# An LSTM step on one core: forget and input gate written to PSUM, and a copy of the cell in SBUF

## The chip, the cores and the metric

The kernel runs on one core of a Trainium2 chip. The metric is the device time of one execution, in microseconds. Before the change it is 229.61 us, the median of three runs (229.58 to 229.65).

## The reference

Two recurrent layers run over 128 time steps on 32 sequences with 128 features each, in fp32. Layer 0 is an LSTM, layer 1 a UGRNN cell; each adds its output to its input. Cut to what matters:

```python
# layer 0, per step; xW is x @ Wx + b
a = xw_t + prev_h @ Wh
i = sigmoid(a[:, :H]);  f = sigmoid(a[:, H:2*H]);  o = sigmoid(a[:, 2*H:3*H]);  g = tanh(a[:, 3*H:])
next_c = f * prev_c + i * g
next_h = o * tanh(next_c)
x = x + hs                                  # input of layer 1
# layer 1, per step
m = concatenate([xt, h]) @ weight + bias
g = sigmoid(m[:, :U] + 1.0);  c = tanh(m[:, U:])
h_new = g * h + (1.0 - g) * c
x = x + ys
```

## The kernel before

Everything is held transposed: the 128 features lie on the partitions, the 32 sequences in the free dimension, so each elementwise operation works on a tile of 128x32. The 128 steps run one after the other in Python-unrolled code, sixteen to a body (`BODY`), and every engine has its own list of instructions in program order. Only semaphores join the lists. No planner or scheduler moves anything. In the texts below "position k" of a step s is k = s modulo 8.

**One step s of layer 0.** TensorE adds `h(s-1) @ Wh` to sums that lie in PSUM, one bank for each gate (`gate_banks`, in the order f, i, g, o). The forget gate comes first, as one product in fp32 (`forget_sum`, L262); the other three are made of three products with `h_high` and one with `h_low` each (`high`, L268, and `low`, L272), in the order i, g, o. ScalarE follows with the sigmoid of f into `forget`, the sigmoid of i into every second element of `scan_mul`, the tanh of g into every second element of `scan_add`, and the sigmoid of o into `out_gate` (all L470, through `gates`). All four results lie in SBUF. VectorE's `keep` (L564) multiplies `forget` by the old cell, which it reads in the bank `cell_bank`, into the other elements of `scan_add`. `scan` (L570) is a `tensor_tensor_scan` over 64 elements that computes i*g + f*c and writes `cell_bank`. ScalarE's `state` (L489) takes the tanh of the cell into `tanh_c`, in the bank `act_bank` of PSUM, and VectorE's `hidden` multiplies it by the output gate, into `hT` (L577) and, scaled and in fp16, into `h_high` (L578). `hidden_low` (L584) makes `h_low`. With `hT` TensorE can begin the next step.

**Layer 1 lies one step behind.** ScalarE takes one tanh over 128x64 (L494, into `acts1`), VectorE makes two `pair1` rows (L591, L593), the new state (L599, `acts<-pair`) and its two remainders (L605 `u_rest`, L610 `u_low`); TensorE multiplies them (L288), each as soon as its part is there. VectorE's list in one step is: hT, h_high, x1T (L619, the sum that feeds layer 1), h_low, the two pair rows, outT (L627, the output), the layer-1 state, keep, u_rest, scan, u_low. `keep` and `scan` therefore stand behind four instructions that wait for layer 1.

**Work for later steps.** TensorE also computes `x @ Wx` for groups of steps ahead, one projection a step (`project0`, L230): into the bank of f at positions 0 and 1, of i at 2 and 3, of g at 4 and 5, of o at 6 and 7. It stands between L288 on `acts` and L288 on `u_rest`. A matmul must not write a bank that another engine is using, so it waits: at positions 0 and 1 for `f_ready` (the forget gate's activation is done), at 2 to 5 for `scan_in_ready` (counted by `keep` and by the activation of g), at 6 and 7 for `o_ready` (the output gate's activation is done). At positions 1 and 3, and at 0 of every second group, it waits for an input chunk (`x_in`) too.

SyncE loads x and stores the output, 64 KB at a time; nothing below depends on it.

Of the kernel before, what the change touches and what calls it, by code (L numbers as in the profile page):

```python
# [8 lines left out]
ACT = mybir.ActivationFunctionType  # L9

P = 128
# [29 lines left out]
def two_layer_recurrence(nc, xt, h_first, wx, wh, b, w1, out_t):  # L41
# [5 lines left out]
    with ctx:  # L47
        def sb(name, shape, dt=F32):
            return ctx.enter_context(nc.sbuf_tensor(name, shape, dt))

        def bank(name):
            return ctx.enter_context(nc.psum_tensor(name, [P, 512], F32))
# [33 lines left out]
        hT = sb("hT", [P, RING, N])  # L86
        h_high = sb("h_high", [P, PARTS, N], F16)
        h_low = sb("h_low", [P, PARTS, N], F16)
        scan_mul = sb("scan_mul", [P, N, 2])
        scan_add = sb("scan_add", [P, N, 2])  # L90
        forget = sb("forget", [P, N])
        out_gate = sb("out_gate", [P, N])


# [10 lines left out]
        cell_bank, act_bank = bank("cell_bank"), bank("act_bank")  # L105
        cell = cell_bank[:, 0:2 * N].rearrange("p (n two) -> p n two", two=2)
        tanh_c = act_bank[:, 0:N]
        a1 = [bank(f"a1_{i}") for i in range(2)]

        x_in = [sem(f"x_in{i}") for i in range(CHUNKS)]  # L110
# [115 lines left out]
        def _(pe):  # L226
# [28 lines left out]
            def first_state(q, done):  # L255

                nc.tensor.matmul(gate_step(q, 0), wh_raw[:, q * P:(q + 1) * P], condT[:, :],  # L257
                                 start=False, stop=True, skip_group_check=True).then_inc(done, 1)
# [7 lines left out]
            def high(q, j):  # L266
                for weights in parts_of(wh_scaled, wh_rest, wh_third, q - 1):
                    nc.tensor.matmul(gate_step(q, j), weights, h_high[:, (j - 1) % PARTS, :],  # L268
                                     start=False, stop=False, skip_group_check=True)
# [59 lines left out]
            bias0(GATE_G, 0, 5)  # L329
            pe.wait_ge(wh_in, 16)  # L330
            pe.wait_ge(cond_in, 16)
            first_state(GATE_I, i_summed)
            first_state(GATE_G, g_summed)
            project0(GATE_O, 0, 7)
            bias0(GATE_O, 0, 7)
            first_state(GATE_O, o_summed)
# [1 line left out]
            def body(s0, first, last):  # L338
                for j in range(BODY):
                    s, m, k = s0 + j, j // GS, j % GS  # L340
                    r, l = s - 1, (j - 1) % BODY
                    if not (first and j == 0):
                        pe.wait_ge(h_ready, s)
                        forget_sum(j)
                        if first and j == 1:
                            pe.wait_ge(wh_split, 2)
                        pe.wait_ge(high_ready, s)
                        high(GATE_I, j)
                        if first and j == 1:
                            pe.wait_ge(fp16_ready, 1)  # L350
                        pe.wait_ge(low_ready, s)
                        low(GATE_I, j, i_summed)
                        high(GATE_G, j)
                        low(GATE_G, j, g_summed)
                        high(GATE_O, j)
                        low(GATE_O, j, o_summed)
                        if first and j == 1:
                            pe.wait_ge(w1_gate_ready, 1)
                            project1(0, 0, 0, 0)
                            project1(1, 0, 0, 0)  # L360
                            bias1(0, 0)
                            pe.wait_ge(w1_scaled, 1)
                            pe.wait_ge(w1_split, 2)
                            pe.wait_ge(fp16_ready, 2)
                            layer1_input(l)
                            layer1_first()
                        else:

                            pe.wait_ge(acts1_ready, s - 1)
                            if first and j == 2:  # L370
                                project1(0, 0, 1, HS)
                                bias1(0, 1)
                                pe.wait_ge(w1_split, 4)
                            if first and j == 3:
                                project1(1, 0, 1, HS)
                            layer1_input(l)
                            layer1_high(r, l)
# [5 lines left out]
                    if k == 0:  # L383
                        if m == 0:
                            pe.wait_ge(x_in[0], s0 + 16)
                            pe.wait_ge(x_in[1], s0 + 16)

                        if not (first and j == 0):
                            pe.wait_ge(f_ready, s)
                        project0(GATE_F, a, a_steps)  # L390
                    if k == 1:
                        if not ends:
                            pe.wait_ge(x_in[2 if m == 0 else 4], s0 + 16)
                        pe.wait_ge(f_ready, s)
                        project0(GATE_F, b, b_steps, False)
                    if k == 2:
                        pe.wait_ge(scan_in_ready, 2 * s + 1)
# [50 lines left out]
        def _(act):  # L448
# [23 lines left out]
            def gates(s, j, first):  # L472
                if not first:
                    act.wait_ge(f_summed, s)
                    gate(forget[:, :], GATE_F, j, ACT.Sigmoid).then_inc(f_ready, 1)
                act.wait_ge(i_summed, s + 1)
                gate(scan_mul[:, :, 1], GATE_I, j, ACT.Sigmoid)
                act.wait_ge(g_summed, s + 1)
                gate(scan_add[:, :, 0], GATE_G, j, ACT.Tanh).then_inc(scan_in_ready, 1)
                if first:  # L480
                    act.wait_ge(w1_in, 16)
                    scale_input(0)
                    scale_input(1).then_inc(w1_scaled, 1)
                act.wait_ge(o_summed, s + 1)
                gate(out_gate[:, :], GATE_O, j, ACT.Sigmoid).then_inc(o_ready, 1)

            def state(s):
                act.wait_ge(cell_ready, s + 1)
                nc.scalar.activation(tanh_c[:, :], cell[:, :, 1], ACT.Tanh).then_inc(tanh_c_ready, 1)  # L489

            def layer1(r, j):
                i = (j - 1) % RING
# [22 lines left out]
        def _(dve):  # L515
# [6 lines left out]

            for slot in range(SLOTS):
                nc.vector.memset(blank[:, slot:slot + 1], 0.0).then_inc(out_free[slot], 16)
            nc.vector.memset(scan_mul[:, :, :].rearrange("p n two -> p (n two)"), 0.0)
            nc.vector.memset(scan_add[:, :, :].rearrange("p n two -> p (n two)"), 0.0).then_inc(zeros_ready, 1)
            then(nc.vector.memset(bias_lhs[:, :], 0.0))
            nc.vector.memset(bias_lhs[ONE_ROW:P, :], 1.0)
# [32 lines left out]

            def keep(s):
                dve.wait_ge(f_ready, s)
                nc.vector.tensor_tensor(scan_add[:, :, 1], forget[:, :], cell[:, :, 1],  # L564
                                        ALU.mult).then_inc(scan_in_ready, 1)

            def scan(s):

                dve.wait_ge(scan_in_ready, 2 * s + 1)
                nc.vector.tensor_tensor_scan(cell[:, :, :].rearrange("p n two -> p (n two)"),  # L570
                                             scan_mul[:, :, :].rearrange("p n two -> p (n two)"),
                                             scan_add[:, :, :].rearrange("p n two -> p (n two)"),
                                             0.0, ALU.mult, ALU.add).then_inc(cell_ready, 1)

# [137 lines left out]
```

## Time and profile before

| what | value |
|---|---|
| median of three runs | 229.61 us |
| span of the profiled execution | 227.5 us, so some 2.1 us of the time lie outside it |
| PE busy | 222.5 us (98%) |
| DVE busy | 200.2 us (88%) |
| ACT busy | 120.1 us (53%) |
| chain that ended last | DVE 79%, ACT 11%, PE 3% |

The busy shares are to be read with care: instructions of one engine overlap in the records. A VectorE instruction lasts some 0.19 us, and the next one on the engine starts some 0.10 to 0.12 us after it did. So two neighbours both count as busy, and an engine can wait for a tenth of a microsecond without an idle record. For a kernel of such small instructions the starts in the timeline say more than the busy time does. The TensorE clock was granted in full (0.997 of 2.4 GHz on average).

### The profile page before, as it was taken

To read this page: it belongs to the slowest core of one execution; us is meant where nothing else is said; L and a number is where in the kernel's file an instruction comes from. 1 tells how busy PE (TensorE), PEld (TensorE's weight loads), DVE (VectorE), ACT (ScalarE), POOL (GpSimd) and SP (SyncE) were. 2 spreads that over 40 slices of the span, in tenths; PEclk is the share of its full clock that TensorE was granted. 3 is DMA by queue.
4 is the path that set the end of the run, shared out by engine and by line. 5 is a ranking of instruction groups with operands and counts; after the bars stand their busy time and mean duration, and the time that the engine had idled before them with its cause. 6 is when DMAs were issued, how large, how long until landed. Compare 5 with 4: busy or idle time off the path is not lost.

```text
span 227.5 us, 12371 instructions
## 1 busy us (share of the span) xinstructions
PE 222.5 (98%) x4850; PEld 207.1 (91%) x4850; DVE 200.2 (88%) x1555; ACT 120.1 (53%) x775; POOL 3.7 (2%) x12
## 2 busy tenths in 40 slices
PE   7999999999999999999999999999999999999994
PEld 5899999999999999999999999999999999999883
DVE  5889889899899898998998989989989989899895
ACT  3555555555555555555555555555555555555551
POOL 2400000000000000000000000000000000000000
PEclk9999999999999999999999999999999999999998
DMA  6001001000010001000011100100001000000000
GB/s 191 23 13 27 19 23 49 17 25 27 20 45 26 26 16 50 26 16 26 26 39 26 27 18 23 49 14 27 27 23 42 26 26 16 27 14 16 14 14 14
DMA packets 12004, 6.69 MB, mean 29 GB/s; under 512 B 1446, under 2 KB 11692, under 8 KB 11948
## 3 DMA queue, kind: packets, MB, share of 16 engines
q1 hardware_dynamic: 11376, 5.33, 8.3%
q8 instruction: 38, 0.62, 1.2%
q10 hardware_dynamic: 572, 0.59, 0.7%
q14 instruction: 18, 0.15, 0.2%
HBM read 3.82 MB, written 2.10 MB: 26 GB/s over the span
## 4 chain that ended last, share of the span: by engine, by line
DVE 79%; ACT 11%; issue 4%; PE 3%; DMA 1%; ACTq 0%
DVE cell_bank L570 13%; ACT act_bank L489 10%; DVE hT L577 8%; DVE scan_add L564 8%; DVE x1T L619 7%; DVE acts L599 7%; DVE pair L591 7%; DVE h_high L578 6%; DVE u_rest L605 6%; DVE outT L627 6%; DVE pair L593 6%; DVE h_low L584 6%; DMA xT<-in_x_dram 1%; PE a L288 1%; PE a L316 0%
## 5 line engine op out<-in xcount | busy, mean ns | idle before, releaser
L262 PE MATMUL gate_f<-hT,wh_raw 128*128 128x32 f32 x254 | 48.0, 271 | 0.3 <-DVE hT L577 0.2
L262 PEld LDWEIGHTS gate_f<-hT,wh_raw 128*128 128x128 f32 x254 | 37.8, 188 | 11.0 <-DVE hT L577 9.3
L470 ACT ACTIVATE forget<-gate_f 128x32 f32<-128x32 f32 x127 | 25.1, 197 | 36.1 <-PE gate_f L262 36.1
L494 ACT ACTIVATE acts<-a 128x64 f32<-128x64 f32 x128 | 28.6, 223 | 29.2 <-PE a L288 28.3
L577 DVE TENSOR_TENSOR hT<-out_gate,act_bank 128x32 f32<-128x32 f32 x128 | 24.0, 187 | 20.9 <-ACT act_bank L489 20.9
L489 ACT ACTIVATE act_bank<-cell_bank 128x32 f32<-128x32 f32 x128 | 23.3, 182 | 35.2 <-DVE cell_bank L570 35.1
L570 DVE TENSOR_TENSOR_SCAN cell_bank<-scan_mul,scan_add 128x64 f32<-128x64 f32 x128 | 38.2, 298 | 0.1
L280 PE MATMUL a<-h_high,w1x_scaled 128*128 128x32 f16 x256 | 35.4, 176 | 0.3 <-DVE w1x_fp L560 0.2
L280 PE MATMUL a<-h_high,w1x_third 128*128 128x32 f16 x256 | 35.4, 176 | 0.0
L280 PE MATMUL a<-h_high,w1x_rest 128*128 128x32 f16 x256 | 35.4, 176 | 0.0
L282 PE MATMUL a<-h_low,w1x_fp 128*128 128x32 f16 x256 | 35.3, 176 | 0.0
L288 PE MATMUL a<-acts,w1h_scaled 128*128 128x32 bf16 x254 | 33.2, 181 | 0.0
L288 PE MATMUL a<-acts,w1h_rest 128*128 128x32 bf16 x254 | 32.1, 177 | 0.0
L288 PE MATMUL a<-acts,w1h_third 128*128 128x32 bf16 x254 | 32.0, 177 | 0.0
L288 PE MATMUL a<-u_rest,w1h_scaled 128*128 128x32 bf16 x254 | 29.3, 178 | 0.0
L288 PE MATMUL a<-u_rest,w1h_rest 128*128 128x32 bf16 x254 | 28.9, 177 | 0.0
L470 ACT ACTIVATE scan_mul<-gate_i 128x32 f32<-128x32 f32 x128 | 25.7, 201 | 0.7 <-PE gate_i L257 0.7
L288 PE MATMUL a<-u_low,w1h_scaled 128*128 128x32 bf16 x254 | 25.9, 178 | 0.1
L470 ACT ACTIVATE scan_add<-gate_g 128x32 f32<-128x32 f32 x128 | 25.7, 200 | 0.0
L280 PEld LDWEIGHTS a<-h_high,w1x_scaled 128*128 128x128 bf16 x256 | 24.8, 97 | 0.8 <-ACT w1h_scaled L466 0.4
L619 DVE TENSOR_TENSOR x1T<-hT,xT 128x32 f32<-128x32 f32 x128 | 25.3, 198 | 0.0
L470 ACT ACTIVATE out_gate<-gate_o 128x32 f32<-128x32 f32 x128 | 25.2, 197 | 0.1
(113 smaller groups left out, 1047.5 us busy)
## 6 DMA issues: line engine op xcount, KB each, us to landing
xT<-in_x_dram SPq DMA_DIRECT2D x45, 64.0 KB, 1.9
out_dram<-outT SPq DMA_DIRECT2D x32, 64.0 KB, 1.6
wx_s<-in_L_cond_Wx_dram SPq DMA_DIRECT2D x1, 256.0 KB, 2.8
wh_raw<-in_L_cond_Wh_dram ACTq DMA_DIRECT2D x1, 256.0 KB, 3.3
w_raw<-in_L_cond_weight_dram ACTq DMA_DIRECT2D x1, 256.0 KB, 3.4
xT<-in_x_dram ACTq DMA_DIRECT2D x1, 64.0 KB, 3.3
bias_rows<-in_biases_dram ACTq DMA_DIRECT2D x1, 3.0 KB
condT<-in_cond_dram SPq DMA_DIRECT2D x1, 16.0 KB, 3.1
```

The costliest lines, as they stand in the source:

```text
L262: nc.tensor.matmul(gate_step(GATE_F, j), wh_raw[:, GATE_F * P:(GATE_F + 1) * P], hT[:, (j - 1) % RING, :], start=False, stop=True, skip_gr ...
L280: nc.tensor.matmul(to, weights, h_high[:, j % PARTS, :], start=False, stop=False, skip_group_check=True)
L282: nc.tensor.matmul(to, w1x_fp16[:, q * P:(q + 1) * P], h_low[:, j % PARTS, :], start=False, stop=False, skip_group_check=True)
L288: mm = nc.tensor.matmul(a1_step(j)[:, q * N:(q + 1) * N], weights, moving, start=False, stop=parts == 1, skip_group_check=True)
L470: return nc.scalar.activation(out, gate_step(q, j), func)
L489: nc.scalar.activation(tanh_c[:, :], cell[:, :, 1], ACT.Tanh).then_inc(tanh_c_ready, 1)
L494: nc.scalar.activation(acts1[:, 0:3:2, i, :], a1_step(j).rearrange("p (g n) -> p g n", g=2), ACT.Tanh).then_inc(acts1_ready, 1)
L564: nc.vector.tensor_tensor(scan_add[:, :, 1], forget[:, :], cell[:, :, 1], ALU.mult).then_inc(scan_in_ready, 1)
L570: nc.vector.tensor_tensor_scan(cell[:, :, :].rearrange("p n two -> p (n two)"), scan_mul[:, :, :].rearrange("p n two -> p (n two)"), scan_ ...
L577: nc.vector.tensor_tensor(hT[:, j % RING, :], out_gate[:, :], tanh_c[:, :], ALU.mult).then_inc(h_ready, 1)
L591: nc.vector.scalar_tensor_tensor(out=pair1[:, 0, :], in0=acts1[:, 0, i, :], scalar=1.0, in1=acts1[:, 1, i, :], op0=ALU.add, op1=ALU.mult)
L619: nc.vector.tensor_tensor(x1T[:, i, :], hT[:, i, :], xT[:, j * N:(j + 1) * N], ALU.add).then_inc(x1_ready, 1)
```

## The change

Forget gate and input gate are written to PSUM in place of SBUF. `forget` takes 32 columns of the forget gate's own bank that its eight steps of sums leave free; `scan_mul` takes 64 columns of `act_bank`, beside `tanh_c`. ScalarE gets one instruction more a step: behind the tanh of the cell it copies the cell to `cell_kept` in SBUF, and `keep` multiplies that by `forget` in PSUM, so that it has one operand in PSUM as before. The order of the gates i and g is changed on TensorE and on ScalarE: g before i, and the activation of i now counts `scan_in_ready`. Because `keep` now reads the forget gate's bank, the projections at positions 0 and 1 wait for `scan_in_ready` in place of `f_ready`.

```diff
-        scan_mul = sb("scan_mul", [P, N, 2])
-        forget = sb("forget", [P, N])
+        cell_kept = sb("cell_kept", [P, N])
...
+        spare = GS * N
+        forget = gate_banks[GATE_F][:, spare:spare + N]
+        scan_mul = act_bank[:, N:3 * N].rearrange("p (n two) -> p n two", two=2)
...
-                        high(GATE_I, j)
+                        high(GATE_G, j)
...
+                        low(GATE_G, j, g_summed)
+                        high(GATE_I, j)
                         low(GATE_I, j, i_summed)
-                        high(GATE_G, j)
-                        low(GATE_G, j, g_summed)
...
                         if not (first and j == 0):
-                            pe.wait_ge(f_ready, s)
+                            pe.wait_ge(scan_in_ready, 2 * s + 1)
                         project0(GATE_F, a, a_steps)
...
-                        pe.wait_ge(f_ready, s)
+                        pe.wait_ge(scan_in_ready, 2 * s + 1)
                         project0(GATE_F, b, b_steps, False)
...
-                    gate(forget[:, :], GATE_F, j, ACT.Sigmoid).then_inc(f_ready, 1)
+                    gate(forget, GATE_F, j, ACT.Sigmoid).then_inc(f_ready, 1)
+                act.wait_ge(g_summed, s + 1)
+                gate(scan_add[:, :, 0], GATE_G, j, ACT.Tanh)
                 act.wait_ge(i_summed, s + 1)
-                gate(scan_mul[:, :, 1], GATE_I, j, ACT.Sigmoid)
-                act.wait_ge(g_summed, s + 1)
-                gate(scan_add[:, :, 0], GATE_G, j, ACT.Tanh).then_inc(scan_in_ready, 1)
+                gate(scan_mul[:, :, 1], GATE_I, j, ACT.Sigmoid).then_inc(scan_in_ready, 1)
...
                 nc.scalar.activation(tanh_c[:, :], cell[:, :, 1], ACT.Tanh).then_inc(tanh_c_ready, 1)
+                nc.scalar.activation(cell_kept[:, :], cell[:, :, 1], ACT.Copy)
...
-                nc.vector.tensor_tensor(scan_add[:, :, 1], forget[:, :], cell[:, :, 1],
+                nc.vector.tensor_tensor(scan_add[:, :, 1], forget, cell_kept[:, :],
                                         ALU.mult).then_inc(scan_in_ready, 1)
```

ScalarE's list over one step, in the middle of the program. Names are out<-in; what an instruction waits for stands in brackets. Before:

```order
L470 ACTIVATE forget<-gate_f 128x32 [waits f_summed]
L470 ACTIVATE scan_mul<-gate_i 128x32 [waits i_summed]
L470 ACTIVATE scan_add<-gate_g 128x32 [waits g_summed]
L470 ACTIVATE out_gate<-gate_o 128x32 [waits o_summed]
L489 ACTIVATE act_bank<-cell_bank 128x32 [waits cell_ready]
L494 ACTIVATE acts<-a_1 128x2x32 [waits a1_summed]
```

Now:

```order
L473 ACTIVATE gate_f<-gate_f 128x32 [waits f_summed]
L473 ACTIVATE scan_add<-gate_g 128x32 [waits g_summed]
L473 ACTIVATE act_bank<-gate_i 128x32 [waits i_summed]
L473 ACTIVATE out_gate<-gate_o 128x32 [waits o_summed]
L492 ACTIVATE act_bank<-cell_bank 128x32 [waits cell_ready]
L493 ACTIVATE cell_kept<-cell_bank 128x32
L498 ACTIVATE acts<-a_1 128x2x32 [waits a1_summed]
```

The first and third activation now write PSUM, g and i have changed places, and the copy stands between the tanh of the cell and the tanh of layer 1.

TensorE's list at position 1, from the last products with the layer-1 state to those with its remainder. Before:

```order
L288 MATMUL a_0<-acts,w1h_rest 128x32
L288 MATMUL a_0<-acts,w1h_third 128x32
L230 MATMUL gate_f<-xT,wx_s 128x128 [waits f_ready,x_in2]
L288 MATMUL a_0<-u_rest,w1h_scaled 128x32 [waits u_rest_ready]
L288 MATMUL a_0<-u_rest,w1h_rest 128x32
```

Now:

```order
L291 MATMUL a_0<-acts,w1h_rest 128x32
L291 MATMUL a_0<-acts,w1h_third 128x32
L233 MATMUL gate_f<-xT,wx_s 128x128 [waits scan_in_ready,x_in2]
L291 MATMUL a_0<-u_rest,w1h_scaled 128x32 [waits u_rest_ready]
L291 MATMUL a_0<-u_rest,w1h_rest 128x32
```

Nothing moves here; the projection waits for a later event, and layer 1's products stand behind it.

## Rows read from the trace of the kernel before

**Rows 1.** The waits: engine, line, who is waited for; us in total, times, longest.

```profile
ACT forget L470 <- PE gate_f L262: 36.1, 126, 0.4
ACT act_bank L489 <- DVE cell_bank L570: 35.1, 126, 0.5
```

**Rows 2.** ScalarE's and VectorE's groups by shape: busy us, mean ns | idle before.

```profile
L470 ACT ACTIVATE scan_mul<-gate_i 128x32 f32<-128x32 f32 x128 | 25.7, 201 | 0.7 <-PE gate_i L257 0.7
L470 ACT ACTIVATE forget<-gate_f 128x32 f32<-128x32 f32 x127 | 25.1, 197 | 36.1 <-PE gate_f L262 36.1
L489 ACT ACTIVATE act_bank<-cell_bank 128x32 f32<-128x32 f32 x128 | 23.3, 182 | 35.2 <-DVE cell_bank L570 35.1
L454 ACT ACT_TABLE_LOAD x1 | 1.3, 1283 | 2.7 <-issue 2.7
...
L570 DVE TENSOR_TENSOR_SCAN cell_bank<-scan_mul,scan_add 128x64 f32<-128x64 f32 x128 | 38.2, 298 | 0.1
L619 DVE TENSOR_TENSOR x1T<-hT,xT 128x32 f32<-128x32 f32 x128 | 25.3, 198 | 0.0
L577 DVE TENSOR_TENSOR hT<-out_gate,act_bank 128x32 f32<-128x32 f32 x128 | 24.0, 187 | 20.9 <-ACT act_bank L489 20.9
L605 DVE TENSOR_TENSOR u_rest<-acts 128x32 f32<-128x32 f32 x127 | 23.7, 186 | 0.0
```

**Rows 3.** VectorE's timeline: start us, us, instruction. One step, and hT eight steps later.

```profile
119.66 0.19 DVE L577 TENSOR_TENSOR hT<-out_gate,act_bank 128x32 f32<-128x32 f32 x1 [0.16 <-ACT act_bank L489]
...
120.42 0.19 DVE L599 SCALAR_TENSOR_TENSOR acts<-pair 128x32 f32<-128x32 f32 x1
120.58 0.19 DVE L564 TENSOR_TENSOR scan_add<-forget,cell_bank 128x32 f32<-128x32 f32 x1
...
120.80 0.30 DVE L570 TENSOR_TENSOR_SCAN cell_bank<-scan_mul,scan_add 128x64 f32<-128x64 f32 x1
...
133.16 0.19 DVE L577 TENSOR_TENSOR hT<-out_gate,act_bank 128x32 f32<-128x32 f32 x1 [0.16 <-ACT act_bank L489]
```

**Rows 4.** ScalarE's timeline over the same step.

```profile
120.35 0.20 ACT L470 ACTIVATE forget<-gate_f 128x32 f32<-128x32 f32 x1 [0.32 <-PE gate_f L262]
...
120.56 0.20 ACT L470 ACTIVATE scan_add<-gate_g 128x32 f32<-128x32 f32 x1
...
121.13 0.18 ACT L489 ACTIVATE act_bank<-cell_bank 128x32 f32<-128x32 f32 x1 [0.27 <-DVE cell_bank L570]
121.55 0.22 ACT L494 ACTIVATE acts<-a 128x64 f32<-128x64 f32 x1 [0.24 <-PE a L288]
```

**Rows 5.** TensorE's weight loads for projections: positions 1, 2, 3 and 6.

```profile
117.45 0.30 PEld L230 LDWEIGHTS gate_f<-xT,wx_s 128*128 128x128 f32 x2
119.13 0.30 PEld L230 LDWEIGHTS gate_i<-xT,wx_s 128*128 128x128 f32 x2
120.88 0.30 PEld L230 LDWEIGHTS gate_i<-xT,wx_s 128*128 128x128 f32 x2
...
125.97 0.30 PEld L230 LDWEIGHTS gate_o<-xT,wx_s 128*128 128x128 f32 x2
```

**Rows 6.** ScalarE's timeline around the projection into the bank of o.

```profile
125.72 0.20 ACT L470 ACTIVATE out_gate<-gate_o 128x32 f32<-128x32 f32 x1
...
126.64 0.22 ACT L494 ACTIVATE acts<-a 128x64 f32<-128x64 f32 x1 [0.26 <-PE a L288]
127.09 0.20 ACT L470 ACTIVATE forget<-gate_f 128x32 f32<-128x32 f32 x1 [0.23 <-PE gate_f L262]
```

**Rows 7.** VectorE's timeline in the step behind that projection.

```profile
126.41 0.19 DVE L577 TENSOR_TENSOR hT<-out_gate,act_bank 128x32 f32<-128x32 f32 x1 [0.17 <-ACT act_bank L489]
...
127.22 0.19 DVE L599 SCALAR_TENSOR_TENSOR acts<-pair 128x32 f32<-128x32 f32 x1
127.33 0.18 DVE L564 TENSOR_TENSOR scan_add<-forget,cell_bank 128x32 f32<-128x32 f32 x1
...
128.10 0.19 DVE L577 TENSOR_TENSOR hT<-out_gate,act_bank 128x32 f32<-128x32 f32 x1 [0.17 <-ACT act_bank L489]
```

More of the change, by code:

```diff
@@ L331, in _ @@
             pe.wait_ge(cond_in, 16)
+            first_state(GATE_G, g_summed)
             first_state(GATE_I, i_summed)
-            first_state(GATE_G, g_summed)
             project0(GATE_O, 0, 7)
@@ L524, in _ @@
                 nc.vector.memset(blank[:, slot:slot + 1], 0.0).then_inc(out_free[slot], 16)
-            nc.vector.memset(scan_mul[:, :, :].rearrange("p n two -> p (n two)"), 0.0)
+            nc.vector.memset(scan_mul.rearrange("p n two -> p (n two)"), 0.0)
             nc.vector.memset(scan_add[:, :, :].rearrange("p n two -> p (n two)"), 0.0).then_inc(zeros_ready, 1)
@@ L570, in scan @@
                 nc.vector.tensor_tensor_scan(cell[:, :, :].rearrange("p n two -> p (n two)"),
-                                             scan_mul[:, :, :].rearrange("p n two -> p (n two)"),
+                                             scan_mul.rearrange("p n two -> p (n two)"),
                                              scan_add[:, :, :].rearrange("p n two -> p (n two)"),
```

## The prediction

> **What bounds the kernel now.** I read the page first: PE 98% busy, DVE 88%, ACT 53%, but the chain that ended last runs over DVE for 79%. As neighbours overlap in the records, I went to the waits next. The two largest say that ScalarE waits once a step for the forget gate's sum and once for the cell [rows 1]: the recurrence runs through all three engines, and the question is where a step's time lies. So I read one step in the two timelines, from one hT to the next [rows 3, 4]. Eight steps take 133.16 - 119.66 = 13.50 us, 1.6875 us each, and one is made up like this:
>
> - hT starts at 119.66; the forget activation starts at 120.35, 0.69 later. In between lie hT itself and the fp32 product with it.
> - The activation takes 0.197 [rows 2]. `keep` starts at 120.58, 0.03 after its end. It did not start when VectorE was free: the layer-1 state ahead of it started at 120.42, and where nothing else is waited for the follower comes 0.11 behind, as from 127.22 to 127.33 [rows 7]. Here it is 0.16, so `keep` waited 0.05 for the forget gate.
> - `keep` ends at 120.77 and the scan starts at 120.80. The activation of g, the other input, ends at 120.56 + 0.20 = 120.76. Both are there within 0.01 us of each other: two paths to the scan are nearly tied.
> - The scan takes 0.30, the tanh starts at 121.13, takes 0.182, hT follows at 121.35.
>
> Sum: 0.69 + 0.197 + 0.03 + 0.188 + 0.03 + 0.30 + 0.03 + 0.182 + 0.03 = 1.68. PE's 98% is not in it as a limit: the forget product starts when hT is there.
>
> There is a third path, layer 1. The steps differ in when L494 comes. At position 6, out_gate starts at 125.72 and ends at 125.92; the projection that waits for it starts loading at 125.97, 1.25 after its step's hT (126.41 - 1.69 = 124.72) [rows 5 to 7]. Layer 1's products stand behind it, so L494 comes 0.67 later, at 126.64, 0.23 after the next hT. The state follows 0.58 later, at 127.22, and `keep` at 127.33. The forget gate was ready at 127.09 + 0.20 = 127.29 and would have let it start at 127.32. So here VectorE, behind layer 1, is already the later one by 0.01. It costs nothing yet: that `keep` ran 0.18 in place of 0.19.
>
> **The change part by part.**
>
> *Forget gate to PSUM.* The nearest row for an activation of this shape into PSUM is the tanh of the cell: 182 ns, from PSUM, against 197 for the forget gate into SBUF and 201 for the strided one of i [rows 2]. I take 15 ns off the forget gate. Bounds: 0, as the tanh reads one bank and writes another, where the new forget gate reads and writes the same bank; and 19, the difference for i.
>
> *Input gate to PSUM and last.* If only the forget gate came earlier, g's activation (120.76) would hold the scan after 0.01 us. Now i takes that place and ends at 120.56 + 0.182 = 120.74 to 120.75, while `keep` would end at 120.77 - 0.015 = 120.755. The two stay tied or i is just ahead, so the 15 ns pass. The order of the sums on TensorE only exchanges two equal groups of four products: 0.
>
> *`keep`.* One operand in PSUM before, one in PSUM now; hT with this mix took 187, `keep` 188 [rows 2]. 0.
>
> *The scan reads scan_mul in PSUM.* Not shown by the trace. VectorE's tensor_tensor over 32 elements took 187 with one operand in PSUM, 186 (u_rest) and 198 (x1T) with none [rows 2]. So one operand in PSUM cost between -11 and +1 ns there, for half as many elements. I take 0, from u_rest. For the bounds I double the spread of 12 for twice the elements and let it go both ways: -24 to +24 ns.
>
> The Trainium skill, "VectorE: DVE Perf Modes", section on the TRN2 errata, has a rule against this edit: a fixed 120 cycles for an instruction with a source in PSUM against 58 for one in SBUF, which at its 0.96 GHz is 65 ns. By it the step would be 65 - 15 = 50 ns longer and the kernel 6 us slower, an estimate from that page alone. The trace does not bear it out for tensor_tensor: 187 against 186 and 198 [rows 2]. No row has a scan with a PSUM source.
>
> *The copy of the cell.* One more ScalarE instruction a step, 124 and more of them, at most 0.20 each by the forget gate's row. It starts some 0.10 behind the tanh's start (121.13), so 121.23 to 121.43; L494 starts at 121.55 [rows 4]. Hidden with 0.12 to spare. L494's own wait is for TensorE. If that cover were gone, layer 1 would come later by what is missing, at most 0.08. The kernel already runs a copy behind the sigmoid with one table load in all [rows 2], so no reload. `keep` needs the copy only a whole step later.
>
> *Positions 0 and 1 wait for scan_in_ready.* Behind that wait on TensorE stand the load for the projection, the products with u_rest and u_low, and then ScalarE's L494 and VectorE's pair, state and `keep`. Position 1's load started 117.45 - 116.29 = 1.16 after its hT. Position 2, which already waits for scan_in_ready, also had 119.13 - 117.97 = 1.16; position 3, which waits for it and an input chunk, had 120.88 - 119.66 = 1.22 [rows 5] (hT taken back from 119.66 by 1.69 each). So position 1 becomes like position 3. As scan_in_ready itself comes 0.015 earlier, 1.205. L494 follows 0.67 later, at 1.875, which is 0.20 after an hT that comes after 1.672; the state at 0.78, `keep` possible from 0.89. The forget gate allows 0.69 + 0.182 + 0.03 = 0.902. Hidden, by 0.01. Position 3 itself now has 121.55 - 121.35 = 0.20 too and keeps it. Position 0 likewise.
>
> *Position 6, what is late next.* o_ready is not made earlier relative to hT: its sum and its activation stay. L494 comes at 1.25 + 0.67 = 1.92, and with a step of 1.672 that is 0.245 after the next hT in place of 0.23. State at 0.825, `keep` at 0.935, against 0.902 in the other steps: 0.033 late, 0.030 when I take off some ns for the shorter `keep`. This one step in eight gets some 1.70 us and not 1.672. At position 7 L494 then falls at 1.92 - 1.70 = 0.22, `keep` at 0.907: 0.002 to 0.005 late.
>
> *Start and end.* The copy in the first steps lies behind instructions that nothing waits for at once; the tail has no gate. 0.
>
> *Sum.* Per eight steps: 8 x 0.0155 = 0.124 less 0.032 held back by the output gate's projection = 0.092. Some 124 steps run at this pace: 15.5 x 0.092 = 1.4 us. The profiled execution would go from a span of 227.5 to 226.1, and with the same 2.1 us outside it, the time from 229.61 to 228.2.
>
> **The rivals.**
>
> *A. The full gain.* Position 6 gives way too (VectorE's list has slack I don't see): 124 x 0.0155 = 1.9 us, 227.7 us. Against it: `keep` was already held by the state there [rows 7].
>
> *B. Nothing.* An activation that reads and writes one bank saves nothing, or the scan takes 10 to 15 ns more and eats it: 229.6 us. For it: no row has either. Against it: the tanh's 182 is a steady mean over 128.
>
> *C. Slower.* The scan's read of PSUM costs more than it saves. At the bound of 24 ns the chain gets 24 - 15.5 = 8.5 ns longer, 124 x 0.0085 = 1.05 us, 230.7 us. It decides from about 13 ns: position 6 is 30 ns behind the others anyway, so seven steps in eight pay x, and 7x = 92 gives 13. For it: the scan is in the chain in every step with nothing beside it. Against it: 187 against 186 and 198 [rows 2]. The skill's rule above is this rival at a larger price.
>
> *D. The change does not do what it says*: the copy or the later projections reach `keep` at other positions than 6. Half of the steps late by 0.015 to 0.03 would bring 228.7 to 229.3. For it: the slack at positions 0, 1 and 3 is only 0.01.
>
> **How the numbers follow.** Forecast 0.44, A 0.16, B 0.12, C 0.14, D 0.14. A measurement can tell about 0.2% here, that is 229.15 to 230.07. Forecast, A and most of D lie below it, some of B as well: faster 0.72. Same 0.13, B and what touches it. Slower 0.15, C. Range 227.3 to 229.9: its low end is A with 4 ns more for activation or scan, its high end takes in B and the mild half of C. The likeliest case alone has 227.9 to 228.6.
>
> **What would show it.** Forget activation 182 to 184 ns in place of 197, the same for i. `keep` 187 to 188. The scan within 5 ns of 298; if it is over 310, C. hT to hT over eight steps 13.40 to 13.42 us in place of 13.50, with seven at 1.67 and one, behind position 6, at 1.70. Position 1's projection loading 1.20 to 1.21 after hT. L494 never behind the copy. The prediction is wrong if the forget activation still takes 197, or if steps other than position 6's are longer than 1.68.

## The result, and the profile after

The changed kernel takes 228.51 us, the median of five runs, against 229.61 us before: a ratio of 0.9949 with a 95% interval of 0.9938 to 0.9961. Forecast were 228.2 us. The span of the profiled execution went from 227.5 to 226.2 us; forecast were 226.1. Some executions of these kernels, the kernel before too, are 4 us late by the end of their fourth step and then run like the others; ratios, spans and times here leave them out (the median of five has one, and is 228.47 without it), and of a trace of one only the later steps are read.

The groups of the changed kernel by shape, as in [rows 2] (busy us, mean ns | idle before):

```profile
L473 ACT ACTIVATE out_gate<-gate_o 128x32 f32<-128x32 f32 x128 | 25.9, 203 | 0.1
L493 ACT ACTIVATE cell_kept<-cell_bank 128x32 f32<-128x32 f32 x128 | 24.7, 193 | 0.0
L473 ACT ACTIVATE act_bank<-gate_i 128x32 f32<-128x32 f32 x128 | 24.3, 190 | 0.0
L473 ACT ACTIVATE gate_f<-gate_f 128x32 f32<-128x32 f32 x127 | 23.1, 182 | 34.2 <-PE gate_f L265 34.2
...
L574 DVE TENSOR_TENSOR_SCAN cell_bank<-act_bank,scan_add 128x64 f32<-128x64 f32 x128 | 38.0, 297 | 0.1
L568 DVE TENSOR_TENSOR scan_add<-gate_f,cell_kept 128x32 f32<-128x32 f32 x127 | 24.2, 190 | 0.4 <-ACT gate_f L473 0.4
```

In the kernel before `keep` had this row:

```profile
L564 DVE TENSOR_TENSOR scan_add<-forget,cell_bank 128x32 f32<-128x32 f32 x127 | 23.8, 188 | 0.4 <-ACT forget L470 0.4
```

The forget gate fell from 197 to 182 ns, the 15 ns of the forecast. The input gate fell from 201 to 190. The scan with `scan_mul` in PSUM took 297 against 298, so the open price was nothing. `keep` took 190 against 188.

The same step as in [rows 3, 4], first ScalarE's timeline, then VectorE's (start us, us, instruction):

```profile
119.77 0.18 ACT L473 ACTIVATE gate_f<-gate_f 128x32 f32<-128x32 f32 x1 [0.29 <-PE gate_f L265]
119.88 0.20 ACT L473 ACTIVATE scan_add<-gate_g 128x32 f32<-128x32 f32 x1
119.98 0.19 ACT L473 ACTIVATE act_bank<-gate_i 128x32 f32<-128x32 f32 x1
...
120.54 0.18 ACT L492 ACTIVATE act_bank<-cell_bank 128x32 f32<-128x32 f32 x1 [0.26 <-DVE cell_bank L574]
120.63 0.19 ACT L493 ACTIVATE cell_kept<-cell_bank 128x32 f32<-128x32 f32 x1
120.96 0.22 ACT L498 ACTIVATE acts<-a 128x64 f32<-128x64 f32 x1
```

```profile
119.08 0.19 DVE L581 TENSOR_TENSOR hT<-out_gate,act_bank 128x32 f32<-128x32 f32 x1 [0.16 <-ACT act_bank L492]
...
119.84 0.19 DVE L603 SCALAR_TENSOR_TENSOR acts<-pair 128x32 f32<-128x32 f32 x1
119.98 0.19 DVE L568 TENSOR_TENSOR scan_add<-gate_f,cell_kept 128x32 f32<-128x32 f32 x1
...
120.21 0.30 DVE L574 TENSOR_TENSOR_SCAN cell_bank<-act_bank,scan_add 128x64 f32<-128x64 f32 x1
...
120.75 0.19 DVE L581 TENSOR_TENSOR hT<-out_gate,act_bank 128x32 f32<-128x32 f32 x1 [0.17 <-ACT act_bank L492]
```

From the first hT, at 119.08, to `keep` are 0.90 us (0.92 before), to the scan 1.13 (1.14), to the next hT 1.67 (1.69). `keep` and the input gate's activation both end at 120.17, so the two paths to the scan are still tied. In the mean over the 75 steps at positions 0 to 4 `keep` ends 4 ns after the activation and the scan starts 34 ns after `keep`'s end, as in the kernel before: `keep` is still the later of the two. The copy ends at 120.82 and layer 1's tanh starts at 120.96.

And the step behind position 6, as in [rows 5 to 7]; the load for the projection, ScalarE's part, then VectorE's:

```profile
125.35 0.30 PEld L233 LDWEIGHTS gate_o<-xT,wx_s 128*128 128x128 f32 x2
```

```profile
125.10 0.20 ACT L473 ACTIVATE out_gate<-gate_o 128x32 f32<-128x32 f32 x1
...
126.02 0.22 ACT L498 ACTIVATE acts<-a 128x64 f32<-128x64 f32 x1 [0.17 <-PE a L291]
126.46 0.18 ACT L473 ACTIVATE gate_f<-gate_f 128x32 f32<-128x32 f32 x1 [0.22 <-PE gate_f L265]
```

```profile
125.78 0.19 DVE L581 TENSOR_TENSOR hT<-out_gate,act_bank 128x32 f32<-128x32 f32 x1 [0.17 <-ACT act_bank L492]
...
126.61 0.19 DVE L603 SCALAR_TENSOR_TENSOR acts<-pair 128x32 f32<-128x32 f32 x1
126.71 0.18 DVE L568 TENSOR_TENSOR scan_add<-gate_f,cell_kept 128x32 f32<-128x32 f32 x1
126.83 0.19 DVE L609 TENSOR_TENSOR u_rest<-acts 128x32 f32<-128x32 f32 x1
126.94 0.29 DVE L574 TENSOR_TENSOR_SCAN cell_bank<-act_bank,scan_add 128x64 f32<-128x64 f32 x1
...
127.48 0.19 DVE L581 TENSOR_TENSOR hT<-out_gate,act_bank 128x32 f32<-128x32 f32 x1 [0.16 <-ACT act_bank L492]
129.16 0.19 DVE L581 TENSOR_TENSOR hT<-out_gate,act_bank 128x32 f32<-128x32 f32 x1 [0.16 <-ACT act_bank L492]
```

The forget gate's activation ends at 126.64 and would let `keep` start at 126.67; the layer-1 state started at 126.61, and `keep` comes 0.10 behind it, at 126.71. The scan, at 126.94, starts 0.05 after `keep`'s end but 0.11 behind `u_rest`, the next on VectorE's list: here it stands behind that list and not behind `keep`'s result. This step takes 127.48 - 125.78 = 1.70 us. The next takes 1.68.

Over long stretches the comparison is finer than the hundredths of a row. From hT of step 6 to hT of step 126 are 15 rounds of eight steps. In the kernel before:

```profile
18.36 0.19 DVE L577 TENSOR_TENSOR hT<-out_gate,act_bank 128x32 f32<-128x32 f32 x1 [0.16 <-ACT act_bank L489]
...
221.04 0.19 DVE L577 TENSOR_TENSOR hT<-out_gate,act_bank 128x32 f32<-128x32 f32 x1 [0.16 <-ACT act_bank L489]
```

That is 13.51 us a round. In the changed kernel:

```profile
18.33 0.19 DVE L581 TENSOR_TENSOR hT<-out_gate,act_bank 128x32 f32<-128x32 f32 x1 [0.17 <-ACT act_bank L492]
...
219.80 0.19 DVE L581 TENSOR_TENSOR hT<-out_gate,act_bank 128x32 f32<-128x32 f32 x1 [0.16 <-ACT act_bank L492]
```

That is 13.43 us a round, 0.081 less. Fifteen such rounds make 1.2 of the 1.3 us by which the span fell; the first steps take as long as before. The round is the measure for the experiments too. Two more traces of the changed kernel gave 13.44, so a difference under 0.01 says nothing.

### The profile page after: what moved, and what is told of

Same layout as the page of the kernel before. It is cut to its first block, busy times and chain, and to the rows that moved or that the text cites. A ratio compares the mean times of both kernels' runs of the same rounds, so it can differ in the third digit from the quotient of the medians.

```text
span 226.2 us, 12499 instructions
## 1 busy us (share of the span) xinstructions
PE 221.1 (98%) x4850; PEld 206.6 (91%) x4850; DVE 198.8 (88%) x1555; ACT 134.1 (59%) x903; POOL 3.7 (2%) x12
## 4 chain that ended last, share of the span: by engine, by line
DVE 79%; ACT 11%; issue 4%; PE 3%; DMA 1%; ACTq 0%
DVE cell_bank L574 13%; ACT act_bank L492 11%; DVE hT L581 8%; DVE pair L595 7%; DVE x1T L623 7%; DVE acts L603 7%; DVE scan_add L568 7%; DVE h_high L582 6%; DVE u_rest L609 6%; DVE outT L631 6%; DVE pair L597 6%; DVE h_low L588 6%; DMA xT<-in_x_dram 1%; PE a L291 1%; PE a L283 0%
## 5 line engine op out<-in xcount | busy, mean ns | idle before, releaser
L265 PE MATMUL gate_f<-hT,wh_raw 128*128 128x32 f32 x254 | 47.0, 267 | 0.3 <-DVE hT L581 0.2
L473 ACT ACTIVATE gate_f<-gate_f 128x32 f32<-128x32 f32 x127 | 23.1, 182 | 34.2 <-PE gate_f L265 34.2
L574 DVE TENSOR_TENSOR_SCAN cell_bank<-act_bank,scan_add 128x64 f32<-128x64 f32 x128 | 38.0, 297 | 0.1
L473 ACT ACTIVATE out_gate<-gate_o 128x32 f32<-128x32 f32 x128 | 25.9, 203 | 0.1
L291 PEld LDWEIGHTS a<-u_rest,w1h_scaled 128*128 128x128 bf16 x254 | 25.0, 99 | 0.1
```

What stands on the lines that cost most here:

```text
L265: nc.tensor.matmul(gate_step(GATE_F, j), wh_raw[:, GATE_F * P:(GATE_F + 1) * P], hT[:, (j - 1) % RING, :], start=False, stop=True, skip_gr ...
L291: mm = nc.tensor.matmul(a1_step(j)[:, q * N:(q + 1) * N], weights, moving, start=False, stop=parts == 1, skip_group_check=True)
L473: return nc.scalar.activation(out, gate_step(q, j), func)
```

## The experiments

Ratios are to the kernel before, run beside each on the same chip. "Round" is the mean of the 15 rounds above. The lengths of single steps are means over the same 15 rounds, from the starts of hT in the trace; they are good to 1 or 2 ns.

| kernel | round, us | step behind position 6, 7, others | ratio, 95% interval |
|---|---|---|---|
| before | 13.51 | 1.692, 1.689, 1.688 | 1 |
| changed | 13.43 | 1.708, 1.676, 1.675 | 0.9949 (0.9938 to 0.9961) |
| input gate back in SBUF | 13.46 | 1.697, 1.680, 1.681 | 0.9973 (0.9958 to 0.9988) |
| input gate's part alone | 13.51 | 1.694, 1.688, 1.687 | 0.9995 (0.9978 to 1.0012) |
| later wait alone | 13.51 | 1.691, 1.687, 1.688 | one run |
| u_rest first at 6 and 7 | 13.46 | 1.693, 1.718, 1.674 | 0.9971 (0.9957 to 0.9984) |
| u_rest first at 6 | 13.43 | 1.695, 1.687, 1.675 | 0.9941 (0.9928 to 0.9954) |
| projections of o into another bank | 13.39 | 1.673, 1.673, 1.675 | 0.9916 (0.9901 to 0.9931) |
| three copies | 13.43 | 1.707, 1.674, 1.675 | 0.9943 (0.9925 to 0.9960) |
| copy behind layer 1's tanh | 13.43 | 1.707, 1.675, 1.675 | one run |
| two banks for o | 13.40 | 1.675, 1.676, 1.675 | 0.9944 (0.9931 to 0.9957) |
| two banks for o, later w1x_third | 13.40 | 1.676, 1.675, 1.676 | 0.9918 (0.9898 to 0.9938) |

The changed kernel ran again beside the two versions with two banks for o, on two chips. What was expected:

> The changed kernel unaltered, beside the version with two banks for o on the same chip. Every theory: span 226.2, steps of 1.674 and 1.707, ratio to the kernel before 0.994 to 0.996.

> The changed kernel unaltered, beside the version with two banks for o and the later w1x_third, on the same chip. Every theory: span 226.2, steps of 1.674 and 1.707, time 228.3 to 228.6.

On the second of these chips the ratio was 0.9946 (0.9931 to 0.9961), with times of 228.51 to 228.71 us and spans of 226.3 to 226.6. On the first there is one time, 228.34 us with a span of 226.2. In both traces the round was 13.44, with steps of 1.675 or 1.676 and, behind position 6, of 1.710 and 1.708.

**Input gate back in SBUF.**

```diff
-        scan_mul = act_bank[:, N:3 * N].rearrange("p (n two) -> p n two", two=2)
+        scan_mul = sb("scan_mul", [P, N, 2])
```

> The changed kernel with scan_mul back in SBUF, all else kept (g before i, i as the last input of the scan, forget gate in PSUM, copy). My theory: the forget gate's 15 ns then meet the activation of i, which ends some 10 ns later than in the changed kernel and starts to hold the scan: scan start moves from 1.128 to 1.133 us behind hT, so steps of 1.680 in place of 1.674 and a span of 226.7 to 227.0. Rival 1: the input gate's place is worth its whole 11 to 19 ns: steps of 1.685 to 1.690, span 227.5 or more. Rival 2: it is worth nothing, all came from the forget gate: steps of 1.674, span 226.2.

Steps of 1.68, and spans of 226.6 to 227.0. My theory held. ScalarE's rows, then VectorE's, of one step, with hT at 123.21:

```profile
124.11 0.20 ACT L473 ACTIVATE scan_mul<-gate_i 128x32 f32<-128x32 f32 x1
```

```profile
124.11 0.19 DVE L568 TENSOR_TENSOR scan_add<-gate_f,cell_kept 128x32 f32<-128x32 f32 x1
...
124.34 0.30 DVE L574 TENSOR_TENSOR_SCAN cell_bank<-scan_mul,scan_add 128x64 f32<-128x64 f32 x1
```

The activation of i ends at 124.31, `keep` at 124.30. The later of the two now is the activation (by 7 ns in the mean over positions 0 to 4), and the scan stands behind it.

**The input gate's part alone.** The kernel before, with `scan_mul` in PSUM and g before i on TensorE and ScalarE.

```diff
-        scan_mul = sb("scan_mul", [P, N, 2])
+        scan_mul = act_bank[:, N:3 * N].rearrange("p (n two) -> p n two", two=2)
...
+                act.wait_ge(g_summed, s + 1)
+                gate(scan_add[:, :, 0], GATE_G, j, ACT.Tanh)
                 act.wait_ge(i_summed, s + 1)
-                gate(scan_mul[:, :, 1], GATE_I, j, ACT.Sigmoid)
-                act.wait_ge(g_summed, s + 1)
-                gate(scan_add[:, :, 0], GATE_G, j, ACT.Tanh).then_inc(scan_in_ready, 1)
+                gate(scan_mul[:, :, 1], GATE_I, j, ACT.Sigmoid).then_inc(scan_in_ready, 1)
```

> The kernel before with only the input gate's part: scan_mul in PSUM, g before i; forget gate in SBUF, no copy, the old waits. My theory: the scan is released by keep, which is released by the forget gate, so nothing is gained: steps of 1.687, span 227.5 (227.4 to 227.6), time 229.6. The scan itself keeps its length of 297 to 300 ns. Rival: the input gate is on the path and gives 5 to 15 ns a step: span 225.7 to 226.9.

Steps of 1.687, span 227.3, ratio 0.9995: nothing that can be told from none, as expected. The two edits are not additive. Per round the input gate's part is worth 0.006 us alone, which is within the spread of one kernel's traces, and 0.030 on top of the forget gate's; the rest of the change gives 0.051 without it. So the path that ends last, `keep`, gains by itself until it meets the other, and only then is an edit of the other worth something. The forget gate in PSUM with g still last was not tried.

Its rows show the price of the scan's read from PSUM by itself, and one effect on the neighbour on ScalarE:

```profile
L570 DVE TENSOR_TENSOR_SCAN cell_bank<-act_bank,scan_add 128x64 f32<-128x64 f32 x128 | 38.0, 297 | 0.1
```

```profile
L470 ACT ACTIVATE out_gate<-gate_o 128x32 f32<-128x32 f32 x128 | 26.0, 203 | 0.1
...
L470 ACT ACTIVATE act_bank<-gate_i 128x32 f32<-128x32 f32 x128 | 24.3, 190 | 0.0
```

**The later wait alone.**

```diff
-                            pe.wait_ge(f_ready, s)
+                            pe.wait_ge(scan_in_ready, 2 * s + 1)
                         project0(GATE_F, a, a_steps)
...
-                        pe.wait_ge(f_ready, s)
+                        pe.wait_ge(scan_in_ready, 2 * s + 1)
                         project0(GATE_F, b, b_steps, False)
```

> The kernel before with only the later wait of the projections at positions 0 and 1 (scan_in_ready in place of f_ready). My theory: position 1's weight load moves from 1.16 to 1.22 us behind hT, layer 1's tanh from 0.15 to 0.20, and keep is not reached: steps of 1.687, span 227.5. Rival: layer 1 is already at its limit at these positions and each such step gets 0.01 to 0.05 us longer: span 227.8 to 229.

Position 1's load stood at 117.42 with its hT at 116.19, 1.23 us (1.16 before), layer 1's tanh came 0.20 after hT and not 0.15, and the steps stayed at 1.688. Span 227.3. Hidden, as forecast.

**u_rest ahead of the projection, at positions 6 and 7.**

```diff
+                    if k in (6, 7) and not (first and j < 2):
+                        layer1_rest(r, l)
                     if k == 6:
                         pe.wait_ge(o_ready, s + 1)
                         project0(GATE_O, a, a_steps)
...
                     if not (first and j < 2):
-                        layer1_rest(r, l)
+                        if k not in (6, 7):
+                            layer1_rest(r, l)
                         layer1_low(r, l)
```

> The changed kernel, with layer 1's products with u_rest put before the projection into the bank of o at positions 6 and 7. My theory: the step behind position 6 is 1.707 us and not 1.674 because layer 1's products stand behind a projection that waits for the output gate. Then the step behind position 6 falls to 1.675 to 1.685, the others stay at 1.674, and the span goes from 226.2 to 225.7 to 225.9 (15.5 steps by 0.02 to 0.03 us). Rival: the wait only changes places (u_low and ScalarE's tanh come as late as before, or the forget product of the next step is now late behind the projection); then the step behind position 6 stays at 1.70 and the span at 226.2 or above.

Both half right, and the spans came to 226.5 to 227.0. Position 6 gave 0.015, not the 0.02 to 0.03 that I expected. Position 7 lost 0.042: its projection started 0.13 us later, TensorE's list ended later, and the next forget product had to wait. The loads for it, and hT before each:

```profile
131.91 0.30 PEld L265 LDWEIGHTS gate_f<-hT,wh_raw 128*128 128x128 f32 x2
...
133.60 0.30 PEld L265 LDWEIGHTS gate_f<-hT,wh_raw 128*128 128x128 f32 x2 [0.17 <-DVE hT L584]
```

```profile
131.64 0.19 DVE L584 TENSOR_TENSOR hT<-out_gate,act_bank 128x32 f32<-128x32 f32 x1 [0.17 <-ACT act_bank L495]
133.36 0.19 DVE L584 TENSOR_TENSOR hT<-out_gate,act_bank 128x32 f32<-128x32 f32 x1 [0.17 <-ACT act_bank L495]
```

0.24 us after hT in the second, 0.27 in the first. As a version it is slower than the changed kernel: 13.46 a round.

**The same at position 6 alone.** The edit above with `(6,)` in place of `(6, 7)`.

> The changed kernel with layer 1's products with u_rest ahead of the projection at position 6 alone. In the run with both positions, position 6 fell from 1.707 to 1.692, but position 7 rose to 1.718 as TensorE's list ended too late for the next forget product. My theory: layer 1 is the chain over positions 6 and 7 together, since its tanh at position 7 comes at a fixed time behind position 6's hT; what 6 gives, 7 takes: 1.692 and 1.688 in place of 1.707 and 1.676, sum 3.38 as now, span 226.2. Rival: position 6's 15 ns are won, with position 7 at 1.676: 15.5 x 0.015 = 0.23 us, span 225.9.

1.695 and 1.687, together 3.382 against 3.384, spans of 226.1 and 226.2, round 13.43. My theory held: layer 1 is one chain over both positions, and what position 6 gives, 7 takes.

**The projections of o into another bank.** The `o_ready` wait and the bank of o are taken away together, at position 7 and for the bias too, with the same products. This kernel leaves out the sums of the reference: what belongs to o is added in the bank of g.

```diff
-                        pe.wait_ge(o_ready, s + 1)
-                        project0(GATE_O, a, a_steps)
+                        pe.wait_ge(scan_in_ready, 2 * s + 1)
+                        project0(GATE_O, a, a_steps, into=GATE_G)
```

> The changed kernel with the projections and the bias of positions 6 and 7 written into the bank of g, behind scan_in_ready, in place of the bank of o behind o_ready. The work on TensorE is the same; the sums of g and o are not the reference's from position 6 on. My theory: position 6's step is long only because its projection waits for the output gate. Then its weight load comes 1.15 us behind hT and not 1.25, layer 1's tanh 0.18 to 0.20 behind the next hT, all steps are 1.674 and the span is 226.2 - 15.5 x 0.035 = 225.7. Rival: TensorE's amount of work at positions 6 and 7 (a projection and two biases in one step) is what makes layer 1 late; then position 6's step stays at 1.70 and the span at 226.2.

Steps of 1.673 to 1.675, round 13.39, spans of 225.5 to 225.9. The load and layer 1's tanh, with hT at 129.42:

```profile
128.89 0.30 PEld L233 LDWEIGHTS gate_g<-xT,wx_s 128*128 128x128 f32 x2
```

```profile
128.75 0.20 ACT L473 ACTIVATE out_gate<-gate_o 128x32 f32<-128x32 f32 x1
...
129.56 0.22 ACT L498 ACTIVATE acts<-a 128x64 f32<-128x64 f32 x1
```

The load starts before the output gate's activation is done (128.95), and the tanh comes 0.14 after hT in place of 0.24, sooner than the 0.18 to 0.20 that I expected. TensorE did the same work, so it was the wait and not the amount of work. Wait and bank were not tried apart.

**Three copies of the cell.**

```diff
                 nc.scalar.activation(cell_kept[:, :], cell[:, :, 1], ACT.Copy)
+                nc.scalar.activation(cell_more[:, 2 * s, :], cell[:, :, 1], ACT.Copy)
+                nc.scalar.activation(cell_more[:, 2 * s + 1, :], cell[:, :, 1], ACT.Copy)
```

> The changed kernel with two more copies of the cell (to tiles that nothing reads) behind the first, so ScalarE has three where it had one. My theory: an instruction on ScalarE follows the one before after 0.09 to 0.10 us, so the three start at 1.55, 1.65 and 1.74 us behind hT, and layer 1's tanh, which comes at 1.82 at the earliest, is pushed at most by some ns at positions with slack: span 226.2 (226.1 to 226.4). Rival: each copy blocks the engine for its 0.19 us; then the third ends at 2.13, layer 1's tanh is 0.1 to 0.3 us late, steps get 0.05 or more longer, and the span is above 232.

Round 13.43, as with one copy. Each starts 0.07 to 0.08 us after the one before:

```profile
119.26 0.19 ACT L494 ACTIVATE cell_kept<-cell_bank 128x32 f32<-128x32 f32 x1
119.33 0.20 ACT L495 ACTIVATE cell_more<-cell_bank 128x32 f32<-128x32 f32 x1
119.41 0.22 ACT L496 ACTIVATE cell_more<-cell_bank 128x32 f32<-128x32 f32 x1
119.55 0.22 ACT L501 ACTIVATE acts<-a 128x64 f32<-128x64 f32 x1
```

The profiled span is 226.5, above the range of my theory. The rounds don't show it; its hT of step 6 stands at 18.66 and not 18.33, and its very first hT at 7.47 and not 7.15, so 0.3 us were lost ahead of the first step's hT. Another execution had a span of 226.0. Why the start varies so was not tried.

**The copy behind layer 1's tanh.** One line moved from `state` to the end of the step.

> The changed kernel with the copy of the cell behind layer 1's tanh in place of ahead of it. My theory: the copy is off the path in both places: steps of 1.674 and 1.707, span 226.2 (226.1 to 226.3). Rival 1: the copy delayed layer 1's tanh at position 6: then its step falls below 1.70 and the span to 226.0 or less. Rival 2: the late copy delays the forget gate's activation: steps longer than 1.68.

1.707 and 1.675, span 226.1, in one run. My theory held, both rivals fell.

**Two banks for o.** The experiments point to a version: take the wait at positions 6 and 7 away and keep the results. `tanh_c` and `scan_mul` move into `cell_bank`; the bank that this frees takes every second group of o. The first projection of o then covers eight steps in place of seven, and the copy of the cell moves behind layer 1's tanh. Cut to what matters:

```diff
-BEGIN = (1, 3, 5, 7)
+BEGIN = (1, 3, 5, 0)
...
+        def gate_bank(q, j):
+            return o_banks[j // GS % 2] if q == GATE_O else gate_banks[q]
...
-                    if k == 6:
-                        pe.wait_ge(o_ready, s + 1)
-                        project0(GATE_O, a, a_steps)
-                    if k == 7 and not ends:
-                        pe.wait_ge(o_ready, s + 1)
-                        project0(GATE_O, b, b_steps, False)
+                    if k == 6 and not ends:
+                        if s > GS:
+                            pe.wait_ge(o_ready, s - 6)
+                        project0(GATE_O, j + 2, HS)
+                    if k == 7 and not ends:
+                        project0(GATE_O, j + 5, HS, False)
...
-                nc.scalar.activation(cell_kept[:, :], cell[:, :, 1], ACT.Copy)
...
+                    if s < T - 1:
+                        act.wait_ge(high_ready, s + 1)
+                        nc.scalar.activation(cell_kept[:, :], cell[:, :, 1], ACT.Copy)
```

> A version of the changed kernel that computes the reference and takes the wait at positions 6 and 7 away. The cell, its tanh and scan_mul share one bank, which frees a bank; the sums of o use two banks in turn, a group of eight steps each (starting at position 0), so the projections for the next group never meet the output gate's activation. The copy of the cell comes behind layer 1's tanh and waits for high_ready, as VectorE reads the tanh in the same bank until then. My theory: every step 1.674, span 225.7 (225.6 to 225.8), the time 0.5 us below that of the changed kernel. Rival 1: the scan reads and writes one bank now and gets longer by some ns: steps of 1.68 and more, span 226.2 or above. Rival 2: the late copy or the longer first projection costs at the start: span 225.8 to 226.2.

All steps 1.675 or 1.676, as my theory had it, but the span stayed at 226.2: the first step took 2.56 us and not 2.13. The place is VectorE's first h_low, beside GpSimd's work on layer 1's weights. VectorE, then GpSimd:

```profile
7.41 0.62 DVE L596 SCALAR_TENSOR_TENSOR h_low<-hT,h_high 128x32 f16<-128x32 f32 x1
```

```profile
7.37 0.61 POOL L182 TENSOR_TENSOR w1x_third<-w1x_rest 128x256 bf16<-128x256 f32 x1
```

In the changed kernel h_low starts at 7.47 and GpSimd's instruction at 7.48, and h_low takes 0.19. In this one GpSimd was first, by 0.04. That this order cost the 0.43 us is what the next run tries.

**The same with w1x_third later.**

```diff
             pool.wait_ge(w1_split, 1)
+            pool.wait_ge(low_ready, 1)
             nc.gpsimd.tensor_tensor(w1x_third[:, :], w1x_rest[:, :], upper(w1x_rest[:, :]),
```

> The version with two banks for o, with one more wait: GpSimd's w1x_third waits for VectorE's first h_low. In the version without it that h_low stood from 7.41 to 8.03 us beside GpSimd's w1x_third (7.37 to 7.98), and the first step took 2.56 us and not 2.13, which cost the 0.43 us that the equal steps had won. My theory: VectorE is held while GpSimd works; with h_low first, it takes 0.19, the first step is 2.13 again, all steps from the fourth on are 1.675, and the span is 225.7 to 225.8, some 0.5 us below the changed kernel. Rival: what held h_low was something else at the start (the copy that waits for h_high, the longer first projection of o); then the first step stays at 2.5 and the span at 226.2.

h_low took 0.19 again, the spans were 225.8 and the two times 227.92 and 227.94 us, a ratio of 0.9918 (0.9898 to 0.9938). That fits my theory; that the first step took 2.13 us again is not shown, as the trace kept of this run can't be compared there. This version is 0.6 us below the lowest time of the changed kernel beside it (228.51), from two executions, and the round, 13.40 against 13.44, says the same.

## Why the prediction was right

- *The chain of a step* was read rightly. Before, the scan hung on `keep`, `keep` on the forget gate, with the other input of the scan 0.01 behind. Both single edits show that tie. They also show that `keep` was the later one, by some 6 ns of the 15: the rest of the change gives 0.051 us a round without the input gate's part.
- *Forget gate to PSUM, 15 ns*: 197 to 182. *`keep`, 0*: it lengthened by 2 in the mean, and by 3, from 189 to 192, in the steps at positions 0 to 4.
- *Input gate to PSUM and last*: I priced it like the tanh, 182, and named 182 to 184 as the sign; it took 190. This cost nothing, as it still ends 4 ns before `keep`. The steps at positions 0 to 4 came to 1.674 and not 1.672: `keep` is 3 ns longer, the scan 1 shorter, and the gain of an ordinary step was 14 and not 15.5 ns.
- *The scan's read*: 0 of a range of -24 to +24, shown by the input gate's part alone. I had no row for it, and that the middle of the range came out was partly luck. The range itself rested on a 198 that is no steady price: `x1T` took 0.59 and 0.56 us in the first two steps, beside GpSimd's work, and 191 to 192 ns in the middle of the program; without those two the spread was 5 ns and not 12. The Trainium skill's rule in "VectorE: DVE Perf Modes" (section on the TRN2 errata), 62 cycles more for a source in PSUM, does not hold for this scan: 297 ns against 298.
- *The copy*: hidden, with more to spare than I said, as the experiments with three and with a late one show.
- *The later wait*: position 1's load at 1.205 forecast; the changed kernel's trace has 116.94 with hT at 115.73, 1.21. Hidden, by the 0.01 or so that I gave it.
- *What is late next*: position 6. Forecast 1.70 for its step and 0.002 to 0.005 lost at 7; measured 1.708 and 0.001 to 0.002. That it is the wait for the output gate, and not TensorE's work, is shown by the projections into another bank. The mis-sized part is small: the output gate's activation grew from 197 to 203 ns behind the strided write of i, so the load came 1.254 us after hT and not 1.25. The longer output gate was seen in every kernel that writes i into PSUM (202 to 203) and in none that does not (197); why was not tried. Two readings were off and cancel in part. I took some ns off for the shorter `keep`, but at position 6 the scan stands behind `u_rest`: it starts 42 ns later than in the steps at positions 0 to 4 and is 8 ns shorter, which makes the 34 between 1.708 and 1.674. And I called the wait free in the kernel before, where its step was already 4 ns longer than the others, 1.692 against 1.688.
- *Sum*: 0.092 a round forecast, 0.081 measured. The missing 0.011 is for the most part the six ordinary steps, by 1.5 to 2 ns each; positions 6 and 7 together were forecast to lose 0.001 and lost 0.002 to 0.003. The round, named as 13.40 to 13.42, came to 13.43. In the time, 1.4 us forecast and 1.1 measured by the medians, 1.3 by the spans.
- Rival A, the full gain, fails at position 6; B and C fail at the groups' means; D fails as no position but 6 has more than 1.678.

## What to carry to other kernels

In a recurrence over several engines, take the starts of one whole step out of the timelines and look for all the paths that meet at an instruction: where two are nearly tied, an edit of the one that ends first is worth nothing alone, an edit of the one that ends last is worth only the distance between them (here 0.051 of the 0.081 us a round), and both together are worth nearly their price. Work out for each position of the schedule what is late once the first path is shorter, since a wait that was just hidden is paid in full then. And buy the next wait off by giving the writer a second bank, not by moving work ahead of the wait: what that gave at position 6 was lost again at position 7.

## What the runs showed of the hardware

- ScalarE's activations of 128x32 fp32: 182 ns from PSUM to PSUM, also where source and destination are in one bank; 190 into every second element of PSUM; 193 for a copy into SBUF, 197 for a gate into SBUF and 200 to 201 into every second element of SBUF; 203 for the gate into SBUF behind the strided write into PSUM.
- In the kernel before, the projection that waits for `scan_in_ready` and an input chunk started its load 1.22 us after hT, where one that waits for `scan_in_ready` alone had 1.16: 0.06 us more at the same event. With the projections of o in another bank, position 0 has 1.21 where it waits for input chunks too and 1.14 where it does not. Which part of the second wait costs this was not tried.
- VectorE's h_low took 0.62 us when a tensor_tensor of GpSimd had started 0.04 before it, and 0.19 when it started 0.01 ahead. The Trainium skill, "SBUF — State Buffer", section on who interferes with whom, has such a lock for a VectorE instruction with two inputs in SBUF against a GpSimd instruction that reads SBUF, where the first to start blocks the other; the trace agrees, with 0.62 against 0.19 us. GpSimd's instruction took 0.61 us where it was first and 0.65 where h_low was. In the kernel before, `x1T` shows the same at the start: 0.59 us where GpSimd's instruction had started 0.07 before it, and 0.19 in the middle of the program.
